# A five-layer cross-attention kernel on one core: one gate matmul for eight, stacks preset by VectorE, the first unit's stacks filled from two queues, another split of PSUM banks, and a written-out order

## The reference, cut to what matters

```python
# phase 0: queries from x, keys and values from the context, RoPE on q and k; x = x + attn @ Wo + bo
# phases 1 and 2 work on x seen as 8 sequences of 128 rows, each with its own conditioning row c:
silu(c) @ ada_w + ada_b -> 9 vectors of 128: shift, scale, gate for three sub-steps
#   phase 1: x = x + gate1 * mha(mod(ln(x), shift, scale))           self-attention
#   phase 2: x = x + gate2 * cross(...); then x = x + gate3 * mlp(mod(ln(x), ...))
# phase 3: x = layernorm(attn(x, context) + x) * g + b
# phase 4: the same with weights quantised to -1, 0, 1 times their mean size; x = x + ...
```

## Time and profile before

| | us |
|---|---|
| median of 3 runs | 359.17 |
| lowest, highest | 354.92, 366.85 |
| the profiled execution | 358.49 |
| its span | 356.7 |
| TensorE busy | 303.9 |
| VectorE busy | 246.3 |
| ScalarE busy | 233.3 |
| GpSimd busy | 187.3 |

### The profile page before, as it was taken

One profiled execution on the slowest core, in us unless ns is written; L12 is line 12 of the kernel. 1 busy time (PEld: TensorE's weight loads), 2 busy tenths in 40 slices (PEclk: granted clock), 3 DMA queues, 4 the chain that ended last, 5 costly groups with the idle time before them and its releaser, 6 DMA issues.

```text
span 356.7 us, 8841 instructions
## 1 busy us (share of the span) xinstructions
PE 303.9 (85%) x3162; PEld 169.3 (47%) x3162; DVE 246.3 (69%) x551; ACT 233.3 (65%) x491; POOL 187.3 (53%) x273
## 2 busy tenths in 40 slices
PE   3187899789899689788988989899888999898993
PEld 2173444345436466556666656455343534344331
DVE  2679599989746657758738487857686879778411
ACT  1131275767878378576768586787787777676782
POOL 3876498968888555336254332403676675740000
PEclk9587699999999899899899989879999999999999
DMA  2769700303032122133132111200212112130000
GB/s 70 184 164 244 249 9 5 83 10 79 16 83 68 33 75 75 50 77 91 27 91 54 39 47 48 60 9 19 74 38 58 51 41 69 37 78 18 17 17 16
DMA packets 40563, 22.95 MB, mean 64 GB/s; under 512 B 4872, under 2 KB 39688, under 8 KB 40392
## 3 DMA queue, kind: packets, MB, share of 16 engines
q1 hardware_dynamic: 39832, 22.30, 23.9%
q0 software_dynamic: 256, 0.07, 0.2%
q10 hardware_dynamic: 432, 0.02, 0.1%
HBM read 5.79 MB, written 0.52 MB: 18 GB/s over the span
## 4 chain that ended last, share of the span: by engine, by line
PE 30%; DVE 6%; ACT 6%; POOL 5%; issue 5%; SPq 1%; DMA 1%; POOLq 0%; ACTq 0%; DVEq 0%
PE ps_small L937 9%; PE ps_heads L937 7%; PE ps_max L937 5%; PE ps_score L937 5%; POOL normed L735 3%; ACT probs L1155 2%; DVE neg_max L1294 2%; PE ps_small L1108 2%; POOL rstd L908 1%; PE ps_small L1112 1%; DVE stats L1258 1%; PE ps_small L1122 1%; SPq L793 1%; DVE normed L735 1%; ACT L1228 1%
## 5 line engine op out<-in xcount | busy, mean ns | idle before, releaser
L1294 DVE TENSOR_REDUCE neg_max<-ps_max 128x2 f32<-128x512 f32 (+1 forms) x256 | 159.8, 682 | 38.4 <-PE ps_max L937 37.7
L1155 ACT ACTIVATE probs<-ps_score 128x512 f32<-128x512 f32 x256 | 141.4, 600 | 29.5 <-PE ps_score L937 28.5
L937 PE MATMUL ps_score<-q_stack,k_stack 64*128 64x256 bf16 (+1 forms) x640 | 78.8, 258 | 6.6 <-ACT probs L1155 4.3
L937 PE MATMUL ps_heads<-probs,v_cols 128*32 128x256 f32 (+1 forms) x1280 | 83.1, 350 | 0.6 <-ACT probs L1155 0.4
L937 PE MATMUL ps_max<-k_stack,q_stack 62*128 62x256 bf16 (+1 forms) x640 | 72.0, 259 | 7.9 <-DVE neg_max L1294 4.1
L937 PEld LDWEIGHTS ps_score<-q_stack,k_stack 64*128 64x128 bf16 x640 | 34.1, 96 | 40.9 <-ACT probs L1155 29.0
L937 PEld LDWEIGHTS ps_max<-k_stack,q_stack 62*128 62x128 bf16 x640 | 33.3, 96 | 41.2 <-DVE neg_max L1294 22.8
L937 PEld LDWEIGHTS ps_heads<-probs,v_cols 128*32 128x32 f32 x1280 | 28.3, 109 | 25.4 <-issue 17.3
L702 POOL TENSOR_TENSOR split_r<-q_f,k_parts 128x256 f32<-128x256 f32 x19 | 12.8, 673 | 46.2 <-issue 41.9
L937 PE MATMUL ps_small<-src_t,w 128*128 128x256 f32 x96 | 30.0, 433 | 0.9 <-issue 0.5
L908 POOL TENSOR_TENSOR rstd<-var_eps,minus_half 128x2 f32<-128x2 f32 x20 | 14.2, 708 | 30.8 <-DVE var_eps L1263 30.6
(11 more groups left out here) (112 smaller groups left out, 420.6 us busy)
## 6 DMA issues: line engine op xcount, KB each, us to landing
k_stack<-k_parts SPq DMA_DIRECT2D x120, 64.0 KB, 2.1
q_stack<-q_parts SPq DMA_DIRECT2D x120, 64.0 KB, 2.1
w<-in_w SPq DMA_DIRECT2D x1, 1024.0 KB, 5.8
rows<-in_rows SPq DMA_DIRECT2D x1, 704.0 KB, 5.0
w<-in_w SPq DMA_DIRECT2D x1, 576.0 KB, 8.6
q_stack<-max_rows SPq DMA_DIRECT2D x36, 8.0 KB
ctx_t<-in_ctx_t SPq DMA_DIRECT2D x4, 128.0 KB, 3.5
src_t<-in_x_t SPq DMA_DIRECT2D x4, 128.0 KB, 3.6
```

The lines of the kernel that those rows point to most:

```text
L937: return nc.tensor.matmul(out, lhs_t, rhs, start=start, stop=stop, **k)
L1155: nc.scalar.activation(probs[:, n % PROB_BUFS, :], ps_score[n % SCORE_BUFS][:, :], ACT.Exp, scale=SCALE).then_inc(exped, 1)
L1294: nc.vector.tensor_reduce(dst, src, AX.X, ALU.max, negate=True).then_inc(max_taken, 1)
```

## The change

- Gates: one step instead of eight. silu(c) itself is the stationary operand, so that the result is 8 rows by 384 columns on 8 partitions; VectorE adds the bias (`gates_once`), one DMA stores it to a new internal DRAM tensor (`gate_store`), and one DMA spreads it to all 128 partitions (`gate_spread`, 12 KB on each partition, 1536 KB in all). `silu_rep`, the copies by ScalarE and GpSimd's additions are gone.
- Stacks preset: the four DMAs of `spare` are gone. VectorE writes zeros over all of `q_stack`, and pairs of bfloat16 ones over all of `k_stack`, before the stacks are first filled (2 memsets of 128x3072 four-byte words).
- Unit 0: its k is split on GpSimd and its q on VectorE. Its k parts are placed from SP's queue and its q parts from ScalarE's. ScalarE copies unit 0's projections (with the bias of q) to `rope_in` ahead, and VectorE reads cosine and sine straight from `ps_heads`.
- GpSimd clears `v_cols` first; the gathers become steps of the order (`gather`), and the loads too (`load`), with w in five groups instead of four.
- Banks: two for maxima and three for scores.
- The planner and its weights are replaced by `ORDER`, a string of 1085 letters, each the next step of one stream.

```diff
-SPARE_SLOTS = (6, 7)
+TWO_ONES = float(np.array([0x3F803F80], np.uint32).view(np.float32)[0])
-SMALL_BUFS, MAX_BUFS, SCORE_BUFS = 2, 3, 2
+SMALL_BUFS, MAX_BUFS, SCORE_BUFS = 2, 2, 3
-SPLIT_ON_DVE = ()
+SPLIT_ON_DVE = (("q", 0),)
...
+def placer(kind, u):
+    return "act" if (kind, u) == ("q", 0) else "sp"
...
+ORDER = (
+    "HRRHPLSPLLDHDRSPDRDPPSRLLDPmHmmLLmmDmmmRRXmmPTSDDYmmPmmGLmmDLGmSDsssmPSsXmsmTsmDsmmGYRmmLPmmsvPvDvGmmsvmssmsmsmsvXsmSm"
...
+        "R": [s for b in range(B) for s in (("expand", b, 0), ("rope", b, 0))],
+        "G": [("small", "mod", 0), ("small", "gate", 0), ("gate_store", 0, 0), ("gate_spread", 0, 0), ("small", "gamma", 0)],
+        "F": [("gate_fold", i, 0) for i in range(2 * B)] + [("quantise", i, 0) for i in range(4)],
+        "L": [("load", name, 0) for name in LOADS],
+        "H": [("gather", b, 0) for b in range(B)],
...
+        def place_parts(engine, kind, u, rest):
+            buf = u % STACK_BUFS
+            if u < STACK_BUFS:
+                engine.wait_ge(stacks_set, 1 if kind == "q" else 2)
+            else:
+                engine.wait_ge(scored, chunks_until(u - STACK_BUFS))
...
-            sp.wait_ge(gathered[0], NT * 16)
-            for kind, stack in ((0, q_stack), (1, k_stack)):
-                for slot in SPARE_SLOTS:
-                    sp.dma_start(stack[slot::ROW_SLOTS, :, :, :].rearrange("r b h t -> r b (h t)"),
...
+                if st[0] == "gate_store":
+                    sp.wait_ge(*used(no("small", "gate", 0)))
+                    sp.dma_start(gate_row.rearrange("(i c) -> i c", i=2 * B), gates_once[:, :, :].rearrange("i g c -> i (g c)")
+                                 ).then_inc(gates_stored, 16)
+                if st[0] == "gate_spread":
+                    sp.wait_ge(gates_stored, 16)
+                    sp.dma_start(gates[:, :, :, :].rearrange("p i g c -> p (i g c)"), gate_row.partition_broadcast(P)
+                                 ).then_inc(gates_spread, 16)
...
-                    link(nc.gpsimd.tensor_tensor(gates[:, i, :, :], gates[:, i, :, :],
-                                                 rows[:, R_AT["gate1"]:R_AT["gate3"] + 1, :], ALU.add))
...
+                    elif b == 1:
+                        pe.wait_ge(roped, 2)
                     else:
-                        pe.wait_ge(rope_ready, b)
+                        pe.wait_ge(rope_ready, b - 1)
...
                     elif kind == "gate":
-                        last = mm(out[:, 0:3 * D].rearrange("p (a b) -> p a b", a=3), silu_rep[:, u, :],
+                        last = mm(out[0:2 * B, 0:3 * D].rearrange("p (a b) -> p a b", a=3), silu[:, 3, :],
                                   w[:, W_AT["ada2"]:W_AT["ada8"] + 1:3, :])
...
+            nc.vector.memset(q_stack[:, :, :, :].rearrange("p r h t -> p (r h t)").bitcast(U32), 0).then_inc(stacks_set, 1)
             table_rows()
...
+            nc.vector.memset(k_stack[:, :, :, :].rearrange("p r h t -> p (r h t)").bitcast(F32), TWO_ONES).then_inc(stacks_set, 1)
```

More of the change, by code:

```diff
@@ L442, in make_schedule @@
-    plan = Plan()
-    plan.done.update({("gathered", u): 9500 + 2600 * u for u in range(B)})
-    plan.done.update({("loads", b): 5500 if b == 0 else 14000 + 1200 * b for b in range(B)})
-    plan.done["silu",] = 32000
-    plan.free.update(dve=5000, pool=20000)
-    at = [0] * len(streams)
-    while True:
-        ready = []
-        for rank, (stream, i) in enumerate(zip(streams, at)):
-            if i < len(stream):
-                t = plan.start(stream[i])
-                if t is not None:
-                    ready.append((t, rank))
-        if not ready:
-            break
-        now = max(plan.free["pe"], min(ready)[0])
-        t, rank = min(ready, key=lambda r: (max(r[0], now) + handicap(r[1], streams[r[1]][at[r[1]]]), r[1]))
-        plan.append(streams[rank][at[rank]], t)
-        at[rank] += 1
@@ L466, in build @@
+    at = {c: iter(stream) for c, stream in streams.items()}
+    steps = [next(at[c]) for c in ORDER]
+    assert len(steps) == sum(map(len, streams.values()))
+    return steps
 def build(nc, a):
@@ L512, in build @@
         q_f = sb("q_f", [P, 2, 2, T])
+        rope_in = sb("rope_in", [P, 2, 2 * T])
         rope_a = sb("rope_a", [P, T])
@@ L548, in build @@
         const_loaded = sem("const_loaded")
-        w_loaded = [sem(f"w_loaded{i}") for i in range(len(W_GROUPS))]
+        w_loaded = {name: sem(f"w_loaded_{name}") for name in W_GROUPS}
         qk_loaded = sem("qk_loaded")
@@ L730, in apply_norm @@
         def apply_norm(engine, ops, u, src):
-            if u and PHASE[u - 1] < 4:
-                engine.wait_ge(small_ready, no("small", "norm_t", u - 1) + 1)
+            if normed_before(u) is not None:
+                engine.wait_ge(small_ready, no("small", "norm_t", normed_before(u)) + 1)
             for qt in range(NT):
@@ L863, in _ @@
             for st in steps:
+                if st[0] == "gather":
+                    b = st[1]
+                    if b == 0:
+                        pool.wait_ge(pos_ready, 1)
+                    for i in range(b * NT, (b + 1) * NT):
+                        nc.gpsimd.indirect_dma_start(rope_rows[:, i, :], None, a["rope"],
+                                                     bass.IndirectOffsetOnAxis(ap=pos_row[:, i:i + 1], axis=0),
+                                                     bounds_check=MAX_POS - 1).then_inc(gathered[b], 16)
                 if st[0] in ("split_q", "split_k") and splitter(st[0][-1], st[1]) == "pool":
@@ L1448, in constants @@
     return {"const": np.eye(P, dtype=np.float32),
-            "rope": np.concatenate([cos, cos, -sin, sin], axis=-1).astype(np.float32), "spare": spare}
+            "rope": np.concatenate([cos, cos, -sin, sin], axis=-1).astype(np.float32)}
 def kernel(**inputs):
```

495 lines of the change are left out of this document (122 added, 373 removed).

## The result

The changed kernel takes 329.12 us, median of 4 runs (328.38 to 333.85), against 359.14 us before (4 runs, 354.92 to 366.85). The ratio is 0.919, with a 95% interval of 0.909 to 0.930: 8% faster. The forecast was 346.5 us and its range 335 to 359 us; the direction was right, the size too small by 17 us, and the time lies outside the range. The profiled execution took 329.49 us, with a span of 327.7 us.

A forecast was written before the change was run, and what follows sets the result against it. The prediction took a waiting start, then VectorE's maxima, then TensorE in fixed order as bounds. Start 3.4, gates 5.5, banks and order 3.0 us, together 11.9 us off 358.5 us, gave 346.6, forecast as 346.5 us; range 335 to 359 us.

The forecast's parts named there:

- What bounds the kernel: Whole kernel: a start waiting on small steps and DMAs, a stretch bound by VectorE's maxima, the rest by TensorE in order.
- The start: Up to the first maxima: they come at 23.2 instead of 26.65 us, 3.4 us gained, ends 0 and 5.0 us.
- I follow it here and keep the 2.3 us inside the range: Start: VectorE's memset does not delay GpSimd's clearing; otherwise the gathers would start 2.3 us late.
- Both are covered: Start: both VectorE memsets, 2.9 us each, lie in waits; the second would cost what it exceeds 4 us by.
- the 6.5 us that I had named as a sign of being wrong: Start: the forecast is wrong if the gathers start past 6.5 us; before, the first started at 5.81 us.
- my better bound: Start: earliest expected first ps_max matmul, 21.7 us; the gain's upper end is 5.0 us, q's second triple directly behind the first.
- The gates: Gate steps: fourteen of sixteen TensorE matmuls go, 7.5 us of its work; 5.5 us gained, ends 2 and 7.5 us.
- placed for costs other than the chip's: New order: the forecast is wrong if a step so placed stands before TensorE for microseconds in each unit.
- Banks and order: Rings of maxima and scores, new order: net gain 3 us, bounded by 14 us gain and 26 us loss.
- More than forecast: Rival: score ring and fixed order give up idle time, 10 us, and gates 7.5 us; 337.6 us, chance 0.18.
- Slower: Rival: with two maximum banks TensorE waits in order for VectorE, 0.1 us at each of 256 maxima; 375.2 us, chance 0.11.
- Absorbed: Rival: the start's gain is used up, gates give only what VectorE leaves, 0 + 2 + 1.5 us; 355 us, chance 0.25.

The follow-up runs named there:

- new_ones_on_act: Changed kernel with the ones of k_stack written by one ScalarE activation instead of the second VectorE memset; 326.22 us.
- new_expand_late: Changed kernel with one letter of the order moved: expand 3 behind max_split 0 1 instead of ahead of max_split 0 0; 328.6 us.
- before_replan23: Kernel before with two maximum and three score banks, the planner making its list for them with weights unchanged; 388.69 us.
- before_warm: Kernel before with five more unused transposes ahead of each of the eight norm_t steps of phases 0 and 1; 353.81 us.
- new_banks22: Changed kernel with two banks for maxima and two for scores, one bank left unused, steps in their places; 356.2 us.

## Why the forecast missed

**What bounds the kernel.** Right in its parts; not seen was that the middle ran in part at half clock. The windows showed 0.93 and 0.91, which is 20.6 us at half clock in 125.8 us, and I passed them over, as I took TensorE's busy time there as work. Part of the 12 us by which TensorE's busy time fell beyond the fourteen matmuls is likely this; it was not measured apart.

**The start** was forecast at 3.4 us and came to 1.9 us at the first maxima. Two steps failed. One is "I follow it here and keep the 2.3 us inside the range": I followed the Trainium skill's rule ("SBUF — State Buffer", section "SBUF: two separate sides") by which a memset doesn't exclude GpSimd, and the gather took 2.4 us longer beside it than before. The measurement decides. The other is "Both are covered": the first memset made the positions 0.88 us late, so that the first gather started past the 6.5 us that I had named as a sign of being wrong. Without the second memset on VectorE (`new_ones_on_act`) the first maxima stand at 22.3 us, near the 21.7 us of my better bound. The memsets' size was right (2.62 us each, 2.9 us taken). The Trainium skill's rule on issuing engines ("DMA: Bandwidth & Descriptors", section "Issuing engines are not separate DMA queues"), which I weighed and turned down, came out nearer for the whole kernel: the issue time was real, at 1.4 us, but at the end nothing of it could be measured.

**The gates**: 5.5 us taken, 5.6 us by the profiled executions and 6.3 us by the medians. With 1.9 us of the start and the 3.8 us of the gates that lie in phase 0, all 5.6 us of phase 0 are accounted for, if they add, and the new order with its banks gave nothing there on balance. That balance holds a loss: the one early letter of `new_expand_late` is worth 4 to 5 us of it in two traces. It is a case of the step "placed for costs other than the chip's" that I had named as a sign of being wrong.

**Banks and order** is the term that was mis-sized: "I take a gain of 3 us". It measured 23.4 - 1.8 (gates after unit 3) = 21.6 us. The reason given for the 3 us, that "TensorE's own idle time is small", failed too: in the whole span, start included, its idle time gave 9.5 us, and its busy time gave 12 us beyond the gates. The error was also to treat two changes as one small net of two large bounds. The bounds were good guides: the mechanism of the loss is what the old order shows, though its size of 46 us is beyond the 26 us; the gain of up to 14 us is near what the score ring lost (11 to 13 us each side). What decides between them is which order meets the banks. The counts of runs that I had made pointed there (64 runs of two maxima and one longer, against 31 runs of three); I wrote that it "is laid for this" and then took a value near zero. They would not have given the size, though, since `before_replan23` has nearly the same runs of maxima and is 60 us slower. The table shows no additive terms: the banks alone lose 46 us, the order with the old banks gains 6.5 us (start and gates are worth about 7.5 us of gain by themselves), both together gain 26.7 us.

**The rivals.** "More than forecast" had the mechanism, the score ring and the fixed order giving up idle time, but its 10 us and so its 337.6 us fell short. "Slower" had its mechanism right, for another kernel: with the old order it costs 46 us. "Absorbed" was wrong about the gates.

**How much of the 21.6 us is clock** stays open within bounds. The middle of the kernel before had 20.6 us at half clock and the changed kernel's has none. If TensorE bounded all of that, it cost 10.3 us. The stretch of `before_warm` in which its groups stand lost about 10 us of half clock and 3.8 us of time. So I estimate 4 to 10 us, a fifth to a half of the 21.6 us, in this pair of executions; the clock differs between executions of the same kernel, so part of that may be chance. The rest is time in which TensorE stood or its work was spread out by waits. That the search itself was needed, rather than any order made for two and three banks, is shown by `before_replan23` only for this planner with these weights. What the old order would give in the new code, start and gates well placed, was not found.

## What to carry to other kernels

Where engines run a fixed common list, the number of banks and the list are one change, and never a sum of two: here the banks alone lost 46 us, the list alone gave about nothing beyond start and gates, and both together some 20 us. The lengths of runs against the banks warn of a loss, but a list with short runs of maxima was still 60 us slower than another, so only a run tells. Read the granted clock by stretch before calling an engine's busy time its work, and read it in more than one execution before crediting an edit with its change. A VectorE fill of 2.62 us beside a GpSimd gather made the gather 2.64 us longer.

## What the runs showed of the hardware that was not expected

- A VectorE memset of 128x3072 four-byte words took 2.62 us, 0.85 ns for each; a GpSimd indirect DMA issued beside it took 3.94 us, and 1.30 us without it. The first memset, of the same size, ran beside GpSimd's memsets of `v_cols` and did not stretch those (0.96 us for 128x1024). The Trainium skill ("SBUF — State Buffer", section "SBUF: two separate sides") tells of GpSimd unable to write descriptors while VectorE runs in a two-port mode. The delay looks like that, but no row shows in which mode the memset ran.
- A cast of 128x8 right after the first memset, at 3.98 us, took 0.87 us, where the same cast took 0.17 us before the change; in `new_ones_on_act`, with the same memset ahead of it, it took 0.84 us. Why is not shown.
- The third score bank, with the order made for it, is worth 27 us of 356 us (`new_banks22` against the changed kernel); the ring of two had shown only 29 us of waiting weight loads, and 4.3 us of TensorE's own.
- The granted clock of TensorE fell to half behind a wait of 1.20 us in one execution and stayed full behind the same wait in another (`before` at 208 us, `before_warm` at 206 us).
